# One row more in each expert's scatter: 96 rows by a second index table, on Trainium2

## What is computed

```python
flat = topk_i.reshape(-1)
oh = jax.nn.one_hot(flat, E, dtype=jnp.int32)
pos = jnp.sum(jnp.cumsum(oh, axis=0) * oh, axis=-1) - 1
slot = flat * C + jnp.minimum(pos, C - 1)
tok = jnp.arange(T * K) // K
buf = jnp.zeros((E * C, H), x.dtype).at[slot].set(x[tok]).reshape(E, C, H)
g = jnp.einsum('ech,emh->ecm', buf, Wg)
u = jnp.einsum('ech,emh->ecm', buf, Wu)
out = jnp.einsum('ecm,ehm->ech', jax.nn.silu(g) * u, Wd).reshape(E * C, H)
yk = out[slot].reshape(T, K, H)
y = jnp.sum(yk * topk_w[..., None].astype(yk.dtype), axis=1)
shared = jax.nn.silu(x @ Sg.T) * (x @ Su.T) @ Sd.T
```

## Time and profile before

| what | value |
|---|---|
| median of 3 runs | 840.81 us (837.95 to 842.42) |
| the profiled execution: its time / its span | 842.78 us / 841.0 us |
| TensorE busy, share of the span | 676.1 us, 80% |
| GpSimd busy | 378.1 us, 45% |
| all scatters on GpSimd (L1229) | 64, 118.2 us, 1847 ns each |
| all gathers on GpSimd (L1222) | 64, 62.3 us, 973 ns each |
| idle of GpSimd just before the scatters | 46.8 us |
| loop over the experts, first transpose to first issue of the last stage | 555.0 to 799.0 us |

### The profile page before, as it was taken

One profiled execution on the slowest core, in us unless ns is written; L12 is line 12 of the kernel. 1 busy time (PEld: TensorE's weight loads), 2 busy tenths in 40 slices (PEclk: granted clock), 3 DMA queues, 4 the chain that ended last, 5 costly groups with the idle time before them and its releaser, 6 DMA issues. The chain is left out here.

```text
span 841.0 us, 16829 instructions
## 1 busy us (share of the span) xinstructions
PE 676.1 (80%) x6353; PEld 482.3 (57%) x6353; DVE 482.0 (57%) x1086; ACT 338.5 (40%) x636; POOL 378.1 (45%) x354
## 2 busy tenths in 40 slices
PE   2699999998988788888745999799999987773083
PEld 1266666676766566665412556477887765553062
DVE  3267776677868777778445999533333332321057
ACT  2477777766767646755121332112222211110000
POOL 5122222125343423431121832847776777776454
PEclk9899999998999989999756999899999999997555
DMA  7234444665532223210018000138999988953298
GB/s 218 27 59 79 79 79 77 99 98 100 100 73 62 47 45 76 48 44 29 5 44 257 2 0 1 42 96 224 239 235 228 231 211 212 225 127 40 24 302 303
DMA packets 125376, 94.30 MB, mean 112 GB/s; under 512 B 73137, under 2 KB 109169, under 8 KB 125297
## 3 DMA queue, kind: packets, MB, share of 16 engines
q1 hardware_dynamic: 96368, 74.57, 35.1%
q0 software_dynamic: 23552, 14.21, 10.2%
q10 hardware_dynamic: 5376, 4.46, 1.7%
HBM read 60.26 MB, written 24.44 MB: 101 GB/s over the span
## 5 line engine op out<-in xcount | busy, mean ns | idle before, releaser
L1229 POOL DMA_INDIRECT sum_d<-nz,tokens x64 | 118.2, 1847 | 46.8 <-issue 14.6
L724 DVE TENSOR_REDUCE mx<-Sc 128x16 f32<-128x1024 f32 x64 | 77.9, 1217 | 37.8 <-PE Sc L401 37.5
L1056 PE MATMUL bank<-xnT,sgu_sb 128*128 128x512 f32 (+1 forms) x192 | 86.9, 601 | 11.8 <-PEq L1588 11.8
L1111 PE MATMUL bank<-xT,wgu_sb 128*88 128x96 f32 x1024 | 95.1, 246 | 0.3 <-ACT xT L1180 0.3
L1279 DVE TENSOR_TENSOR hid<-sil,bank 88x192 f32<-88x192 f32 x64 | 22.4, 350 | 118.2 <-ACT sil L1186 88.6
L1111 PEld LDWEIGHTS bank<-xT,wgu_sb 128*88 128x88 f32 x1024 | 89.4, 157 | 0.6 <-issue 0.5
L600 ACT COPY ET<-ring 128x512 f32<-128x512 f32 x128 | 69.5, 589 | 44.0 <-PE ring L413 41.8
L429 PEld LDWEIGHTS O<-vbd,ET 128*64 128x64 f32 x2048 | 69.2, 142 | 25.9 <-issue 17.3
L413 PE MATMUL ring<-ident,E 128*128 128x128 f32 x512 | 73.8, 290 | 12.5 <-ACT E L639 11.5
L728 DVE TENSOR_TENSOR E<-Sc,mx 128x1024 f32<-128x1024 f32 x64 | 78.4, 1225 | 6.9 <-DVE mx L724 0.5
L401 PE MATMUL Sc<-kbd,qT 64*64 64x256 f32 x1024 | 76.4, 404 | 6.7 <-DMA kbd<-kT 6.7
(11 more groups left out here) (149 smaller groups left out, 1144.1 us busy)
## 6 DMA issues: line engine op xcount, KB each, us to landing
wgu_sb<-in_wgu_dram SPq DMA_DIRECT2D x64, 352.0 KB
wd_sb<-in_wd_dram SPq DMA_DIRECT2D x64, 176.0 KB
sum_d<-zeros SPq DMA_DIRECT2D x16, 524.0 KB, 6.4
y<-sum_d SPq DMA_DIRECT2D x16, 512.0 KB, 8.8
kbd<-kT SPq DMA_DIRECT2D x248, 32.0 KB, 2.1
X<-in_x_dram SPq DMA_DIRECT2D x8, 512.0 KB, 6.4
rows_d<-xhT SPq DMA_DIRECT2D x8, 512.0 KB, 3.0
out_dram<-X ACTq DMA_DIRECT2D x8, 512.0 KB, 5.2
```

The lines of the kernel that those rows point to most:

```text
L724: nc.vector.reduce_max(mx[:, m % 2, :], sc, AX.X).then_inc(s_mx, 1)
L1056: last = nc.tensor.matmul(out[0:m, :], sgu[:, e, k * MS + m0:k * MS + m0 + m], xnT[:, e, TOK * g:TOK * (g + 1)], start=e == 0, stop=e == 1)
L1111: last = nc.tensor.matmul(GP[e % 2][0:MH, CAP * u:CAP * (u + 1)], wgu[:, j, 4 * MH * c + MH * u:4 * MH * c + MH * (u + 1)], xT[:, e % 2, c ...
L1229: pool.indirect_dma_start(w["sums"][e % 2], bass.IndirectOffsetOnAxis(ap=tokens[0:CAP - 1, e:e + 1], axis=0), outs[0:CAP - 1, e % EB, :], ...
```

## The change

The scatter names 96 rows instead of 95, and takes its destinations from a new table `targets`, 96 x 64 integers like `tokens`. Rows 0 to 94 of `targets` equal those of `tokens`. Row 95 is 4096 + 95 = 4191 for every expert, the last padding row of the sums, which nobody reads. It is made by one more VectorE instruction out of the same transposed bank, times `own` plus `lastrow`; `lastrow` is a new constant of 96 values (0, and 4191 for slot 95), set by a memset and a select on GpSimd. GpSimd waits for the second table once, ahead of its loop.

```diff
--- before.py
+++ after.py
@@ -968,10 +968,11 @@
     def sem(name):
         return ctx.enter_context(nc.semaphore(f"m_{name}"))
 
-    X, ident, xnT, key, wt, kw, nz, top2, both, thr, top, tokf, slot, mark, lastk, sg, su, hT, sh, tokens = (
+    X, ident, xnT, key, wt, kw, nz, top2, both, thr, top, tokf, slot, mark, lastk, sg, su, hT, sh, tokens, targets = (
         mem[k] for k in ("X", "ident", "xnT", "keys", "wt", "kw", "nz", "top2", "both", "thr", "top", "tokf", "slot",
-                         "mark", "lastk", "sg", "su", "hT", "sh", "tokens"))
-    xg, xT, sil, hid, wcol, own, lastone = (mem[k] for k in ("xg", "xT", "sil", "hid", "wcol", "own", "lastone"))
+                         "mark", "lastk", "sg", "su", "hT", "sh", "tokens", "targets"))
+    xg, xT, sil, hid, wcol, own, lastone, lastrow = (
+        mem[k] for k in ("xg", "xT", "sil", "hid", "wcol", "own", "lastone", "lastrow"))
     outs = nz[0:CAP, :].rearrange("p (j e) -> p j e", e=E)
     P = mem["banks"]
     sgu, sd, wgu, wd = w["sgu_sb"], w["sd_sb"], w["wgu_sb"], w["wd_sb"]
@@ -1227,8 +1228,8 @@
                 if e >= 2:
                     pool.wait_ge(s_s[e % 2], 16 * (e // 2))
                 pool.indirect_dma_start(w["sums"][e % 2],
-                                        bass.IndirectOffsetOnAxis(ap=tokens[0:CAP - 1, e:e + 1], axis=0),
-                                        outs[0:CAP - 1, e % EB, :], None, compute_op=ALU.add).then_inc(s_s[e % 2], 16)
+                                        bass.IndirectOffsetOnAxis(ap=targets[:, e:e + 1], axis=0),
+                                        outs[:, e % EB, :], None, compute_op=ALU.add).then_inc(s_s[e % 2], 16)
 
             hidden(0)
             nc.gpsimd.tensor_scalar(nz[:], key[:], 0.0, NOKEY, ALU.is_equal, ALU.mult).then_inc(s_nz, 1)
@@ -1241,6 +1242,7 @@
             for e in range(EB):
                 gather(e)
             add(GE - 1)
+            pool.wait_ge(s_list, 2)
             for e in range(NE):
                 if e >= 3:
                     scatter(e - 3)
@@ -1335,6 +1337,8 @@
                                     ALU.mult, ALU.add).then_inc(s_tok, 1)
             dve.wait_ge(s_tt, 1)
             nc.vector.tensor_copy(tokens[:], P[0][0:CAP, 0:NE]).then_inc(s_list, 1)
+            nc.vector.tensor_scalar(targets[:], P[0][0:CAP, 0:NE], own[:], lastrow[:], ALU.mult,
+                                    ALU.add).then_inc(s_list, 1)
 
             dve.wait_ge(s_thr, 2)
             for h in range(2):
@@ -1557,6 +1561,7 @@
 
         mem["banks"] = [pb(f"bank{k}", [128, 512]) for k in range(8)]
         mem["tokens"] = sb("tokens", [CAP, NE], I32)
+        mem["targets"] = sb("targets", [CAP, NE], I32)
         w["sgu_sb"] = sb("sgu_sb", [128, 2, 2 * MS])
         w["sd_sb"] = sb("sd_sb", [128, 3, E])
         w["wgu_sb"] = sb("wgu_sb", [128, EB, 8 * MH])
@@ -1583,7 +1588,7 @@
                             ("mark", [128, CAP]), ("lastk", [128, 5]), ("sg", [128, 3, TOK]), ("su", [128, 3, TOK]),
                             ("hT", [128, 3, TOK]), ("sh", [128, GT, E]), ("xg", [CAP, EB, E + NE]),
                             ("xT", [128, 2, 2, CAP]), ("sil", [MH, 2, 2 * CAP]), ("hid", [MH, 2, 2, CAP]),
-                            ("wcol", [CAP, EB]), ("own", [CAP, 1]), ("lastone", [CAP, 1])):
+                            ("wcol", [CAP, EB]), ("own", [CAP, 1]), ("lastone", [CAP, 1]), ("lastrow", [CAP, 1])):
             mem[name] = sb(name, shape)
         with nc.Block() as block:
             @block.gpsimd
@@ -1592,8 +1597,10 @@
                                allow_small_or_imprecise_dtypes=True).then_inc(s_iota, 1)
                 nc.gpsimd.memset(mem["own"][:], 1.0).then_inc(s_half, 1)
                 nc.gpsimd.memset(mem["lastone"][:], 0.0).then_inc(s_half, 1)
-                pool.wait_ge(s_half, 2)
-                for m, op, fill in ((mem["own"], ALU.not_equal, 0.0), (mem["lastone"], ALU.not_equal, 1.0)):
+                nc.gpsimd.memset(mem["lastrow"][:], 0.0).then_inc(s_half, 1)
+                pool.wait_ge(s_half, 3)
+                for m, op, fill in ((mem["own"], ALU.not_equal, 0.0), (mem["lastone"], ALU.not_equal, 1.0),
+                                    (mem["lastrow"], ALU.not_equal, float(NT * 128 + CAP - 1))):
                     nc.gpsimd.affine_select(out=m[:], in_=m[:], compare_op=op, fill=fill, base=-(CAP - 1),
                                             pattern=[[0, 1]], channel_multiplier=1).then_inc(s_half, 1)
         moe_phase(nc, ctx, mem, w)
```

## The result

| | before | after |
|---|---|---|
| median of four runs beside each other | 839.45 us (837.95 to 842.42) | 806.44 us (804.97 to 807.75) |
| ratio | | 0.960, 95% interval 0.957 to 0.964 |
| profiled execution: time / span | 842.8 / 841.0 us | 804.97 / 803.2 us |
| the 64 scatters on GpSimd, mean of one | 1847 ns | 1434 ns |
| packets of the software queue | 23552 | 10240 |

The change is worth 33 us, 4.0%. The forecast was 790 with a range of 783 to 812: the time is in the range, 16 us above the point, and outside the likeliest case's own range of 784 to 799. Of some 50 us forecast, two thirds came.

A forecast was written before the change was run, and what follows sets the result against it. GpSimd was taken to bound the kernel from expert 37 to the last scatter, TensorE before, transfers behind 799. Terms -27.4 - 23.3 - 1.7 + 0.2 = -52.2 us gave 790.6 from 842.8, stated as 790, range 783 to 812.

The forecast's parts named there:

- likeliest case: Whole kernel: cheaper 96-row scatters let TensorE bound the loop to its end; 790 us, own range 784 to 799, chance 0.70.
- The largest divisor, packets, no fillers: Scatter layout: 96 rows go six to each of 16 engines without fillers; software queue 10240 packets instead of 23552.
- X = 0.95: GpSimd's time for one 96-row scatter, X, falls from 1.85 to 0.95 us, near a gather's 0.94.
- 320 entries to 112 explains the two durations without it: Argument that GpSimd's entry counts alone explain scatter 1.85 and gather 0.94 us, with no cost for adding.
- pays by rows added: Rival on GpSimd's scatters: X stays 1.85 us and only the landing gets shorter; 815 us, chance 0.10.
- The wait for scatter e-2 allows 1.8 us: GpSimd's loop: with X 0.95 and landing 2.6 us, waiting for the scatter two before permits 1.8 us per round.
- Term 1: Experts 36 to 63: TensorE at its own pace takes 67.35 us instead of 94.74, -27.4 us.
- Term 2: Transposes of expert 63 to the last scatter's end on GpSimd: 7.5 us instead of 30.8, -23.3 us.
- Term 3: Landing of the last scatter: 2.6 us instead of 4.3, -1.7 us.
- The rest of the way to 799.04: From the last scatter's landing to the end of the expert block at 799.04: claimed to stay unchanged.
- Constants (+0.2): Added memset and select on GpSimd between two barriers: +0.2 us; the second table's VectorE instruction hidden by idleness.
- DMA bound: Rival, experts 36 to 55: DMA engines limit the pace to 3.15 us per expert; 802 us, chance 0.13.

The follow-up runs named there:

- e7: Changed kernel with scatters taking only rows 0 to 94 (95 rows, overflow row left out): 840.08 us, ratio to before 1.002.
- e1: Changed kernel with scatters of 96, 95, 92, 91, 90, 80, 64 or 48 rows by expert modulo 8: 814.58 us.
- e2: Changed kernel with scatters that overwrite instead of adding, still 96 rows: 814.64 us.
- e12: e2 repeated word for word on another chip, scatters overwriting instead of adding: 798.42 us.
- e9: Changed kernel with four tables of sums, all cleared, so a scatter waits for scatter e-4 instead of e-2; last stage adds two: 797.13 us.
- e3: Changed kernel loading only half of each gate and up weight block for experts 8 to 63: 809.36 us.
- e4: Changed kernel with four tables of sums, only two cleared, so a scatter waits for scatter e-4; last stage adds two: 808.39 us.

## Why the prediction was right, and where its size was off

1. *The largest divisor, packets, no fillers.* Right: 10240 packets, and e7 and e1 show by their packet counts that 96 rows use 16 engines and 95 use five. That is the rule which the prediction took from the Trainium skill (DMA: Bandwidth & Descriptors, "Why a DMA increments its semaphore by 16 and not by 1"), and the trace agrees.
2. *X = 0.95.* This term was mis-sized: it is 1.43. The step that failed is "320 entries to 112 explains the two durations without it". Of the 0.91 us between the old scatter and a gather, 0.51 is the price of adding (e2, e12) and 0.42 the price of eleven idle engines (e1). The change could take away only the second. The rival "pays by rows added" erred on the other side: X didn't stay at 1.85, and half the rows cost 0.04 us less.
3. *The wait for scatter e-2 allows 1.8 us.* Right in the quiet tail, where the forecast landing of 2.6 us is 2.65 by like rows (744.60 to 747.25). Wrong while weights are loaded, and this is the second term that was mis-sized: the 2.6 came from one gather near the end, and between scatters 45 and 49 the landing took 7 to 8.3 us. A and B are better by 4.6 and 9.1 us without this wait (e9). That the weight transfers are what delays the landing fits these rows and is not shown, since e3 was muddled.
4. *Term 1, experts 36 to 63: -27.4 forecast, -22.6 measured.* TensorE kept its pace to expert 57. That it can keep it to 63 (67.35 forecast) is shown twice, at 67.47 us, once without the wait and once with a cheap scatter. Either of the two suffices; with both costs present 4.65 us are lost: in the three waits, and 1.7 of it in the lower clock behind the first of them.
5. *Term 2, tail: -23.3 forecast, -10.5 measured.* The 12.8 us are the backlog, eleven scatters at 1.98 each behind the last gather. With X = 0.93 and the wait B is 14.3 (e12), with X = 1.44 and without the wait 11.2 (e9), where 7.5 was forecast. So the wait alone costs 6.8 us, the larger X alone 3.7, and both together 12.8: the late landing has the larger share, and neither carries the loss alone.
6. *Term 3: -1.7 forecast, +1.5 measured* from the end of the last scatter to the last stage. The landing is quicker, as said, but "The rest of the way to 799.04" did not stay: GpSimd's drain at the end of the block takes 6.8 us in this trace and 3.8 in that of before.
7. *Constants (+0.2), before expert 36, last stage.* Nothing to be seen of the first. The 5.4 us that the profiled run gained up to expert 36 are not the change's, because e7 with the old row count stands at expert 36 at 661.17 us, within 1 us of it. It also has the last stage at 41.1 us, so the 0.7 there is no effect either. So the profiled execution flatters the change by 5 to 6 us.

Against the sum of 790.6: +4.8, +12.8 and +3.2 for the three terms, -5.4 and -0.7 for what is not the change's, -0.2 for the constants give 805.1; the run took 805.0.

That the time fell into the range is in part luck. The likeliest case had the mechanism of the packets, but its own range ended at 799, and no case of the prediction gives 806. The range reached to 812 to take in the DMA bound (802) and values of X up to 1.8, and what moved the time up was neither the DMA bound nor mainly X. One of the prediction's own signs of being wrong came true as well: TensorE waited for `xg` behind expert 44, three times from expert 58 on.

*The DMA bound* (802) was near in time and wrong in its mechanism: with the engines 0.97 busy in e9, TensorE waited for nothing from expert 36 to 63. If the sharing of the engines acts, it does so by way of the scatters' landing (point 3).

## What to carry to other kernels

An indirect transfer from GpSimd should have a number of rows whose largest divisor up to 16 is 16; a padding row is cheaper than a count that divides badly. A landing time read where nothing else is in the queues (2.65 us here) doesn't hold where transfers are dense (up to 8.3). Before pricing an operation by its neighbour, look for what the neighbour doesn't do (here: adding), and give that its own term. If an engine has a chain behind a start that hardly gets shorter, look at what stands before the start: moving the eight pieces from ahead of expert 0 was worth 15.8 us, of which 7.2 were the earlier start.

## What the runs showed that was not expected

- GpSimd's drain at the end of the expert block, the bulk of D, took 3.8 us in the kernel before, 6.8 after and with four tables, 10.5 with the plain scatter, 3.7 with scatters and 3.3 with gathers of mixed rows (the drain is an instruction of the trace between the last landing and the first issue of the last stage). It repeats to the last digit: 3.822 us in both kernels with 95 rows (before, e7), 10.519 in both runs of the plain scatter, 6.803 in all eight traces with 10240 packets. It isn't longer for more packets (23552 in the kernel before, 6144 with the plain scatter). What sets it wasn't found.
- In four kernels run one after another (e1 to e4), results of TensorE reached ScalarE up to 5.9 us after the last matmul's start with the granted clock at 1.00. One of them repeated word for word (e12) and one with the same expert block (e9) didn't show it and were 16.2 and 11.3 us faster. So it seems to belong to executions and not to a kernel; none of the four was repeated on the same chip, but that chip showed none of it in the next four kernels. What causes it stays open.
- Adding during a scatter takes the joining of rows away: 112 packets against 48 for 96 rows of 1 KB.
